# Second attention: the scores of a batch's first half, issued on TensorE directly behind the outputs of the preceding round

## The chip, the cores and the metric

The kernel runs on one core of one Trainium2 chip. The metric is the device time of one execution in microseconds (us), lower is better. The profile names the engines PE (TensorE matmuls), PEld (TensorE weight loads), DVE (VectorE), ACT (ScalarE), POOL (GpSimd) and SP (SyncE, which issues DMAs here).

## What is computed

Sixteen batches of 128 tokens with 128 features go through two layers, all in fp32. Each layer is a cross-attention over a context of 128 tokens and an expert layer, each behind a layer norm and a residual:

```python
x = x + xattn0(layernorm(x), ctx)      # 16 heads of 8
x = x + ffn0(layernorm(x))             # top 2 of 8 experts
x = x + xattn1(layernorm(x), ctx)      # 16 heads of 64, the "second attention"
x = x + ffn1(layernorm(x))             # 16 experts, each takes 32 tokens of a batch

def xattn1(x, context):                # low-rank terms are folded into the weights
    q_in = x @ Wq                      # 16 heads x 64
    org, ipa = context[:124], context[124:]
    out = attention(q_in, org @ Wk, org @ Wv) + attention(q_in, ipa @ Wk_ipa, ipa @ Wv_ipa)
    return out @ Wo + bo
```

The two attentions of the third line have softmaxes of their own, one over 124 context tokens and one over the last 4.

## The kernel before

Every engine has a program written out by hand, and waits on semaphores for the others; no scheduler reorders anything. The first attention runs from the start to about 139 us of the span, the second attention, together with the first expert layer and the router of the second, to about 393 us, and the second expert layer to the end.

The second attention is a loop of rounds, `round1(b)` for b = -1 to 16, on each engine in its own order. In round b TensorE works on three batches at once: the scores of batch b, the inputs of batch f = b+1 (queries, keys, values) and the end of batch t = b-1 (turning its probabilities, outputs, projection); beside these, one batch g = b+4 of the first expert layer. TensorE's order in round b before the change is: scores of the first half (L1510, heads 0 to 7, banks 0 and 1), turn 0 (L1521), queries 0 (L1530), turn 1, queries 1, expert block (L1463), scores of the second half (L1510, banks 2 and 3), turn 2, keys 0 (L1538), turn 3, expert block, outputs of both halves (L1551), keys 1, values 0 (L1558), inputs (L1564, a transpose), values 1, projection (L1721, bank 7). In rounds 1 and 5 a router of the first expert layer adds a turn (L1451) and logits (L1458) to the first part; in rounds 12 and 13 the second router adds blocks (L1570, L1576, L1583), and in rounds 15 and 16 the gathering of tokens does.

A `scores(b, half)` call is eight matmuls that take 64 rows of the array each, two side by side. It waits for the queries and keys of its half, for the four extra context tokens (`Z.ki`), and for the exponentials of batch b-1 that still read its banks (`Z.exp`).

VectorE's order in a round is: reduce the first quarter of the scores (`shifted(b, 0)`, L772 to L775), copy the turned tile 0 of batch t out of bank 4 (`turned(t, 0)`, L783), the second quarter, turned tile 1, small work on sums and statistics, the third quarter, turned tile 2, the fourth quarter, keys 0 (L919), turned tile 3, expert outputs (L745), the reciprocals and the norm of the four tokens; then it waits for the projection of batch t and does the residual (L306), its statistics (L310), in some rounds further normalizing (L698, L621), and the normalized tile xn of batch b+3 (L301). ScalarE does the exponentials (L1150) and copies queries, keys, outputs and values out of the banks. GpSimd scales the probabilities (L498), adds up the expert outputs (L481, L483) and adds the bias (L492).

Two waits of TensorE matter below. Queries 1 writes bank 4, so it waits until VectorE has copied turned tile 0 out of it; the second half of the outputs waits for turned tile 3:

```python
queries(f, 1, *((Z.p_sb, CH * t + 1) if there(t) else (Z.q_sb, 2 * f)))
...
outputs(t, 1, *p_copied(t, 3))
```

Of the kernel before, what the change touches and what calls it, by code (L numbers as in the profile page):

```python
# [37 lines left out]
def after(eng, sem, value):  # L38

    if not isinstance(value, int) or value >= 1:  # L40
        eng.wait_ge(sem, value)


def there(b):
    return not isinstance(b, int) or 0 <= b < B
# [6 lines left out]
def build_program(nc, T, out):  # L52

    with ExitStack() as ctx:
# [15 lines left out]
        def blocks(b_, rows=128):  # L70
            return b_[0:rows, :].rearrange("p (g n) -> p g n", g=CH)
# [217 lines left out]
        def p_copied(t, n):  # L289

            done = CH * min(t, LAST_TURNS) + 2 * max(t - LAST_TURNS, 0) + n + 1
            if t < LAST_TURNS:
                return Z.p_sb, done
            return (Z.p_odd, 2 * (t - LAST_TURNS) + n // 2 + 1) if n % 2 else (Z.p_sb, done - n // 2)

        def head_of(b):

            return {-1: 1, 1: 2, 5: 3}.get(b)
# [1029 lines left out]
        def _(pe):  # L1328
# [172 lines left out]
            def scores(b, half):  # L1501

                pe.wait_ge(Z.q_sb, 2 * b + half + 1)
                pe.wait_ge((Z.k0_sb, Z.k1_sb)[half], b + 1)
                pe.wait_ge(Z.ki, b + 1)
                after(pe, Z.exp, CH * (b - 1) + 2 * half + 2)
                for c in range(CH):
                    for odd in range(2):
                        rows = slice(D1 * odd, D1 * odd + D1)
                        mm = pe.matmul(blocks(bank[2 * half + odd])[:, c, :], q1T[rows, b % 2, CH * half + c, :],  # L1510
                                       k1T[rows, b % 2, CH * half + c, :], start=True, stop=True)
                        if c == CH - 1:
                            mm.then_inc(Z.score, 1)
# [27 lines left out]
            def outputs(t, n, freed, count):  # L1541

                for k in (2 * n, 2 * n + 1):
                    pe.wait_ge(*p_copied(t, k))
                pe.wait_ge(Z.v_sb, 2 * t + n + 1)
                pe.wait_ge((Z.vi0, Z.vi1)[t % 2], 16 * (t // 2 + 1))
                after(pe, freed, count)
                for c in range(CH):
                    for odd in range(2):
                        h = 8 * n + 2 * c + odd  # L1550
                        mm = pe.matmul(blocks(bank[5 - n])[D1 * odd:D1 * odd + D1, c, :], v1[:, t % 2, D1 * h:D1 * h + D1],  # L1551
                                       p1T[:, CH * (2 * n + odd) + c, :], start=True, stop=True)
                mm.then_inc(Z.o, 1)
# [12 lines left out]
            def route_turn(g, to):  # L1566

                pe.wait_ge(R.xn, 4 * g + 4)
                for k in range(4):
                    mm = pe.transpose(blocks(to)[:, k, :], xn_half[g // 2][:, 4 * (g % 2) + k, :], ident[:, :])  # L1570
                mm.then_inc(R.tr, 1)
# [40 lines left out]
            def round1(b):  # L1612
                f, t, g, j = b + 1, b - 1, b + 4, head_of(b)
                if b == 0:
                    pe.wait_ge(W.taken, ALL_TAKEN)
                    pe.wait_ge(W.added, ALL_ADDED)
                if there(b):
                    scores(b, 0)
                if there(t):
                    turn(t, 0, Z.o_sb, 2 * t)  # L1620
                if b == B:
# [60 lines left out]
                    gather(6)  # L1682
                if there(t):
                    outputs(t, 1, *p_copied(t, 3))
                if b == 12:
                    pe.wait_ge(R.h, 1)
                    route_turn(1, bank[7])
# [94 lines left out]
            for b in range(-1, B + 1):  # L1782
                round1(b)
# [95 lines left out]
```

## Time and profile before

| | |
|---|---|
| time, median of 3 runs | 515.21 us (513.41 to 516.83) |
| span of the profiled execution | 513.1 us |
| PE busy | 487.3 us, 95% of the span |
| DVE busy | 354.2 us, 69% |
| ACT busy | 288.2 us, 56% |
| POOL busy | 234.4 us, 46% |
| chain that ended last, by engine | PE 79%, DVE 12%, ACT 3% |

The page gives the profiled execution by its span, from its first to its last instruction, and no other time of it; the median of the three timed runs is 2.1 us above that span. The page has parts for busy time, for the span in slices, for the chain of work that ended last and for groups of instructions by line. The views used below are the chain in order of time (start, length, what; a piece ends where the next link starts, so its length is what it adds to the chain) and the timeline of one engine (start, length, engine, line, operation, tiles; neighbours of one line are merged, and idle time before a row stands behind it in brackets with what ended it).

### The profile page before, as it was taken

How to read it: one execution, taken by the hardware profiler on the slowest of the kernel's cores; microseconds unless marked ns; L12 is line 12 of the kernel's file. 1: busy time of each engine (PE TensorE's matmuls, PEld its weight loads, DVE VectorE, ACT ScalarE, POOL GpSimd, SP SyncE). 2: the span in 40 equal slices, each digit the busy share in tenths (PEclk: the TensorE clock that was granted, in tenths of full speed). 3: DMA queues.
4: the chain of work that ended last, by engine and by line, in shares of the span. 5: the costliest groups of instructions: out<-in, count | busy, mean ns of one | idle time of the engine just before them, and what ended most of it. 6: DMA issues, size and time to landing. Idle time of an engine off the chain costs nothing.

```text
span 513.1 us, 13570 instructions
## 1 busy us (share of the span) xinstructions
PE 487.3 (95%) x5109; PEld 378.7 (74%) x5113; DVE 354.2 (69%) x1000; ACT 288.2 (56%) x984; POOL 234.4 (46%) x331
## 2 busy tenths in 40 slices
PE   4799999998999999999999999899999999999996
PEld 3466766656668778887787777788757897799995
DVE  5888989766786678566786665757866588535553
ACT  3366566463586776666867657665664444413332
POOL 4845545035365544575444755324231980090440
PEclk9699999999999999999999999999999999999999
DMA  8900000000001100111000000022202100000001
GB/s 229 234 3 4 3 3 3 3 1 8 4 1 32 34 20 16 34 33 34 3 2 2 4 3 3 1 66 64 64 0 71 56 0 1 1 22 24 1 2 42
DMA packets 21872, 14.48 MB, mean 28 GB/s; under 512 B 5928, under 2 KB 21136, under 8 KB 21808
## 3 DMA queue, kind: packets, MB, share of 16 engines
q1 hardware_dynamic: 20704, 13.31, 9.6%
q8 instruction: 42, 0.69, 0.6%
q10 hardware_dynamic: 1104, 0.30, 0.3%
q14 instruction: 22, 0.18, 0.1%
HBM read 12.30 MB, written 1.05 MB: 26 GB/s over the span
## 4 chain that ended last, share of the span: by engine, by line
PE 79%; DVE 12%; ACT 3%; issue 2%; DMA 1%; POOL 1%; ACTq 0%; DVEq 0%; POOLq 0%
PE bank L1792 9%; PE bank L1721 6%; PE bank L1551 5%; PE bank L1558 5%; PE bank L1801 5%; PE bank L1538 5%; PE bank L1510 5%; PE bank L1374 5%; PE bank L1463 5%; PE bank L1521 4%; PE bank L1530 4%; PE bank L1808 3%; PE bank L1609 3%; PE bank L1359 3%; ACT work L1150 2%
## 5 line engine op out<-in xcount | busy, mean ns | idle before, releaser
L1150 ACT ACTIVATE work<-bank,negmax 128x124 f32<-128x124 f32 x256 | 90.0, 387 | 52.2 <-DVE ipa_s L775 52.0
L498 POOL TENSOR_TENSOR work<-work,rsum 128x496 f32<-128x496 f32 x64 | 64.1, 1012 | 120.2 <-DVE rsum L789 120.2
L533 POOL TENSOR_SCALAR work<-work,slot 128x128 f32<-128x128 f32 x64 | 49.7, 792 | 48.3 <-DVE slot L864 29.4
L1150 ACT ACTIVATION_READ_ACCUMULATOR work<-bank,negmax 128x1 f32 x256 | 58.9, 230 | 0.0
L1792 PE MATMUL bank<-work 128*128 128x256 f32 x224 | 53.4, 381 | 0.0
L1014 DVE SCALAR_TENSOR_TENSOR work<-work,bank 128x256 f32<-128x256 f32 x64 | 26.9, 421 | 33.0 <-ACT work L1302 32.8
L1302 ACT ACTIVATE work<-bank 128x256 f32<-128x256 f32 x64 | 24.5, 383 | 40.6 <-PE bank L1792 29.1
L481 POOL TENSOR_TENSOR work<-work 128x512 f32<-128x512 f32 (+2 forms) x48 | 39.2, 817 | 12.1 <-DVE work L745 9.6
L306 DVE TENSOR_TENSOR x_all<-bank,x_all 128x128 f32<-128x128 f32 x16 | 4.7, 292 | 57.4 <-PE bank L1721 55.4
L1792 PEld LDWEIGHTS bank<-work 128*128 128x128 f32 x224 | 40.3, 190 | 4.7 <-DVE work L1017 0.2
L773 DVE TENSOR_REDUCE negmax<-bank 128x4 f32<-128x496 f32 x64 | 42.5, 664 | 0.0
L432 POOL TENSOR_TENSOR rstd<-veps,minus_half 128x1 f32<-128x1 f32 (+3 forms) x28 | 21.2, 755 | 46.1 <-DVE veps L575 45.8
L783 DVE COPY work<-bank 128x512 f32<-128x512 f32 x60 | 40.9, 681 | 0.8 <-PE bank L1521 0.8
L1510 PEld LDWEIGHTS bank<-work 64*128 64x128 f32 x512 | 31.1, 187 | 13.9 <-ACT work L1157 7.6
L629 DVE TENSOR_REDUCE negmax<-bank 128x8 bf16<-128x1024 f32 x32 | 39.1, 1221 | 2.2 <-PE bank L1344 1.7
L1521 PE MATMUL bank<-ident,work 128*128 128x128 f32 x256 | 40.1, 279 | 0.1
L1510 PE MATMUL bank<-work 64*128 64x128 f32 x512 | 37.2, 285 | 1.1 <-issue 1.1
L1090 ACT ACTIVATE work<-bank 128x1024 f32<-128x1024 f32 x32 | 31.0, 1021 | 11.8 <-PE bank L1359 11.8
L1551 PEld LDWEIGHTS bank<-work 128*64 128x64 f32 x512 | 27.7, 136 | 13.5 <-issue 8.7
L1721 PEld LDWEIGHTS bank<-work 128*128 128x128 f32 x256 | 31.1, 192 | 7.4 <-ACT work L1163 5.4
L1530 PE MATMUL bank<-xT,work 128*128 128x128 f32 x256 | 34.3, 278 | 1.6 <-DVE work L783 1.4
L1538 PE MATMUL bank<-cT_all,work 96*128 96x124 f32 x256 | 35.1, 280 | 0.0
(197 smaller groups left out, 1101.1 us busy)
## 6 DMA issues: line engine op xcount, KB each, us to landing
work<-in_L_ffn_w_dram SPq DMA_DIRECT2D x42, 128.0 KB, 2.3
x_all<-in_x_dram SPq DMA_DIRECT2D x4, 256.0 KB, 5.8
out_dram<-x_all SPq DMA_DIRECT2D x4, 256.0 KB, 2.6
ctx_all<-in_ctx_dram SPq DMA_DIRECT2D x4, 192.0 KB, 6.0
ctx_all<-in_L_ffn_w_dram SPq DMA_DIRECT2D x6, 128.0 KB, 2.3
work<-in_L_xattn_Wq_dram SPq DMA_DIRECT2D x1, 512.0 KB, 6.5
work<-in_L_xattn_Wo_dram SPq DMA_DIRECT2D x1, 512.0 KB, 8.2
work<-in_L_ffn_We_dram SPq DMA_DIRECT2D x1, 512.0 KB, 5.7
```

Source lines behind the costliest of these rows:

```text
L498: pool.tensor_tensor(part, part, rsum1[:, b % 2, CH * n:CH * n + CH].unsqueeze(2).broadcast_to((128, CH, ORG)), ALU.mult).then_inc(Z.norm, 1)
L533: ins = pool.tensor_scalar(ohw_of(e)[:, k, :], count[:, :], slot[:, h, 0, k, e % E1:e % E1 + 1], slot[:, h, 1, k, e % E1:e % E1 + 1], ALU. ...
L773: dve.tensor_reduce(negmax1[:, b % 2, part], got_s[:, :, 0:ORG], X, ALU.max, negate=True)
L783: dve.tensor_copy(p1T[:, CH * n:CH * n + CH, :], blocks(bank[(4, 6, 5, 4)[n]])).then_inc(Z.p_sb, 1)
L1150: ins = act.activation(p1[:, b % 2, n, c, 0:ORG], blocks(bank[n])[:, c, 0:ORG], ACT.Exp, bias=negmax1[:, b % 2, h:h + 1], accum_out=sums1[ ...
L1510: mm = pe.matmul(blocks(bank[2 * half + odd])[:, c, :], q1T[rows, b % 2, CH * half + c, :], k1T[rows, b % 2, CH * half + c, :], start=True ...
L1521: mm = pe.transpose(blocks(bank[(4, 6, 5, 4)[n]])[:, c, :], p1[:, t % 2, n, c, :], ident[:, :])
L1530: mm = pe.matmul(blocks(bank[5 - n])[:, c, :], wq1[:, part], xT[:, f % 2, :], start=True, stop=True)
L1538: mm = pe.matmul(bank[6][:, ORG * c:ORG * c + ORG], wk1[0:C, part], cT_all[:, f, 0:ORG], start=True, stop=True)
L1551: mm = pe.matmul(blocks(bank[5 - n])[D1 * odd:D1 * odd + D1, c, :], v1[:, t % 2, D1 * h:D1 * h + D1], p1T[:, CH * (2 * n + odd) + c, :], s ...
L1721: mm = pe.matmul(bank[7][:, 0:D], o1T[:, c, :], wo1[:, c, :], start=(c == 0), stop=(c == 7))
L1792: mm = pe.matmul(halves(bank[4 + c])[:, n, :], up_weights(e, n, c), xgT[e // E1][:, :, e % E1, :], start=True, stop=True)
```

## The change

In rounds 1 to 15 the call `scores(b, 0)` no longer opens round b. It is made one round earlier, in round b-1, behind the second half of the outputs and ahead of the second block of keys. The scores of batch 0 stay where they were. No other engine's program is touched.

```diff
@@ def round1(b), TensorE @@
                 if b == 0:
                     pe.wait_ge(W.taken, ALL_TAKEN)
                     pe.wait_ge(W.added, ALL_ADDED)
-                if there(b):
-                    scores(b, 0)
+                    scores(0, 0)
                 if there(t):
                     turn(t, 0, Z.o_sb, 2 * t)
@@
                 if there(t):
                     outputs(t, 1, *p_copied(t, 3))
+                if f > 0 and there(f):
+                    scores(f, 0)
                 if b == 12:
                     pe.wait_ge(R.h, 1)
                     route_turn(1, bank[7])
```

TensorE's order from the outputs of one ordinary round (L1551) to the second queries block of the next (the second L1530), before the change; each row is a line, its operation and tiles, and how many matmuls:

```order
L1551 MATMUL bank<-work 64x128 x16
L1538 MATMUL bank<-cT_all,work 128x124 x4
L1558 MATMUL bank<-work,cT_all 124x512
L1564 MATMUL bank<-ident,xn 128x128
L1558 MATMUL bank<-work,cT_all 124x512
L1721 MATMUL bank<-work 128x128 x8
L1510 MATMUL bank<-work 128x128 x8
L1521 MATMUL bank<-ident,work 128x128 x4
L1530 MATMUL bank<-xT,work 128x128 x4
L1521 MATMUL bank<-ident,work 128x128 x4
L1530 MATMUL bank<-xT,work 128x128 x4
```

The same stretch after the change (the projection's line is L1722 there):

```order
L1551 MATMUL bank<-work 64x128 x16
L1510 MATMUL bank<-work 128x128 x8
L1538 MATMUL bank<-cT_all,work 128x124 x4
L1558 MATMUL bank<-work,cT_all 124x512
L1564 MATMUL bank<-ident,xn 128x128
L1558 MATMUL bank<-work,cT_all 124x512
L1722 MATMUL bank<-work 128x128 x8
L1521 MATMUL bank<-ident,work 128x128 x4
L1530 MATMUL bank<-xT,work 128x128 x4
L1521 MATMUL bank<-ident,work 128x128 x4
L1530 MATMUL bank<-xT,work 128x128 x4
```

The scores (L1510) moved up over keys, values, inputs and projection; all else keeps its order. VectorE's order around the same place, from the end of one round to the copy that the second queries block waits for, after the change (in brackets the semaphores that a row waits for):

```order
L798 TENSOR_TENSOR work<-ipa_s,ipa_sum 128x16x4 [waits z_ipa_step]
L306 TENSOR_TENSOR x_all<-bank,x_all 128x128 [waits z_xb,z_proj]
L310 BN_STATS stats<-x_all 128x6 [waits z_x_new]
L301 TENSOR_SCALAR xn<-x_all,mv,rstd 128x128 [waits z_tr,ln_rstd]
L772 TENSOR_REDUCE ipa_max<-bank 128x4 [waits z_score]
L773 TENSOR_REDUCE negmax<-bank 128x4
L775 TENSOR_TENSOR ipa_s<-bank,ipa_max 128x16 [waits z_ipa_max]
L783 COPY work<-bank 128x512 [waits z_turned]
```

Nothing moved here: all of VectorE's rows stand as before, the residual (L306) ahead of the scores' reduction (L772).

## Rows read from the trace of the kernel before

**Rows 1.** The page: the span, and busy time by engine.

```profile
span 513.1 us, 13570 instructions
PE 487.3 (95%) x5109; PEld 378.7 (74%) x5113; DVE 354.2 (69%) x1000; ACT 288.2 (56%) x984; POOL 234.4 (46%) x331
```

**Rows 2.** Chain of waits, round 8: start us, length us, what.

```profile
257.48 1.09 PE bank L1510 x16
258.57 0.59 PE bank L1521 x4
...
260.05 0.44 PE bank L1521 x4
260.49 0.89 PE bank L1530 x8
...
263.92 0.89 PE bank L1538 x8
...
266.11 1.90 PE bank L1551 x32
268.01 1.08 PE bank L1538 x8
...
270.93 1.79 PE bank L1721 x16
```

**Rows 3.** Timeline of VectorE, round 8: start us, length us, line, operation.

```profile
257.52 0.29 DVE L306 TENSOR_TENSOR x_all<-bank,x_all 128x128 f32<-128x128 f32 x1 [4.13 <-PE bank L1721]
...
258.06 0.37 DVE L301 TENSOR_SCALAR xn<-x_all,mv,rstd 128x128 f32<-128x128 f32 x1
258.61 0.18 DVE L772 TENSOR_REDUCE ipa_max<-bank 128x4 f32<-128x16 f32 x1 [0.18 <-PE bank L1510]
...
259.36 0.68 DVE L783 COPY work<-bank 128x512 f32<-128x512 f32 x1
...
266.04 0.68 DVE L783 COPY work<-bank 128x512 f32<-128x512 f32 x1
```

**Rows 4.** Chain of waits, the start of round 10.

```profile
287.96 0.02 issue
...
289.26 0.35 DVE xn L301
...
290.97 0.14 issue
291.10 1.13 PE bank L1530 x8
```

**Rows 5.** Chain of waits, round 7.

```profile
241.88 1.14 PE bank L1510 x16
243.02 0.16 DVE ipa_max L772
...
251.69 1.09 PE bank L1551 x16
```

**Rows 6.** Timeline of VectorE, ahead of round 1.

```profile
145.70 2.01 DVE L698 TENSOR_SCALAR work<-x_all,mv,rstd 128x128 f32<-128x128 f32 x2
```

**Rows 7.** Chain of waits, round 1.

```profile
148.31 0.44 PE bank L1451 x4
...
150.87 0.99 PE bank L1530 x8
```

**Rows 8.** Chain of waits, round 13.

```profile
337.53 1.09 PE bank L1510 x16
...
341.40 0.89 PE bank L1530 x8
```

**Rows 9.** Timeline of VectorE, round 14.

```profile
358.78 0.18 DVE L772 TENSOR_REDUCE ipa_max<-bank 128x4 f32<-128x16 f32 x1
```

**Rows 10.** Chain of waits, round 15.

```profile
370.22 2.87 ACT work L1150 x16
```

**Rows 11.** Timeline of GpSimd, round 8.

```profile
258.98 0.45 POOL L492 TENSOR_TENSOR x_all<-x_all,bias 128x128 f32<-128x128 f32 x1
```

## Prediction

> **What bounds the kernel now.** The page comes first: TensorE is busy for 95% of a 513.1 us span [rows 1]. A busy TensorE can still be waiting in disguise, so the chain of waits comes next. I read it over the second attention, where the change lies, and speak of round b from P, the end of the projection that closes round b-1, to the next P. In round 8 (257.48 to the next P, 272.72 = 270.93 + 1.79) every link is a TensorE block that starts when the one before it ends [rows 2]: 15.24 us without a gap. Each block's length is the distance to the next start.
>
> The blocks show a second thing. The first half's scores (L1510) take 1.09 us and the turn behind them 0.59 us, while the same turn behind whole-array work takes 0.44 us. Keys take 1.08 us behind the outputs and 0.89 us elsewhere [rows 2]. Scores use half the array's rows, outputs half its columns; each change of mode costs 0.15 to 0.2 us (0.59 - 0.44, 1.08 - 0.89).
>
> Then the timeline of VectorE in the same round [rows 3]. After P it takes the projection (L306), the statistics, the normalized tile xn (L301, from P + 0.58), and only then reduces the scores (L772, from 258.61, after 0.18 us of waiting for them) and copies the first turned tile (L783). That copy frees bank 4 for the second queries block (L1530 at 260.49). VectorE's order is fixed, and the change leaves it as it is. So today the scores on TensorE (1.09 us) and VectorE's residual and xn (0.9 us) run side by side. VectorE has no long wait until the next P: its last copy for the outputs starts at 266.04, near the outputs themselves.
>
> **What the change costs.** Its instruction count is nil: in rounds 1 to 15 the eight scores matmuls leave the round's head and stand, with their four waits, behind the outputs of the round before. I take head and tail apart.
>
> *Head.* TensorE loses 1.09 us and the 0.15 us of the following turn, 1.24 us. From P it now does turn, queries, turn: 0.44 + 0.89 + 0.44 = 1.77 us, and stands before the second queries block. That block waits for VectorE's copy. How long VectorE needs is shown where it is already the bound: in round 10 xn starts at 289.26 and the block at 291.10, 1.84 us later, with 0.14 us from the copy's end to the matmul [rows 4]. With xn at P + 0.58 the block can start at P + 2.42, not P + 1.77: a stall of 0.65 us. Before, it started at P + 3.01 (260.49 - 257.48). So the head gives 0.59 us, not 1.24. The first block behind such a stall also takes 1.13 us instead of 0.89 [rows 2, 4], 0.24 us more. What was hidden behind the scores (residual, statistics, xn) becomes visible, because the scores no longer stand there.
>
> *Tail.* The block now stands between outputs and keys, where TensorE is the only bound and nothing waits for a scores block: 1.09 us more, less what keys save by following scores (1.08 against 0.89 + 0.15): +1.05 us. No row shows outputs followed by scores. Below, I bound it by a block with no change of mode at all: 16 matmul records of the projection take 1.79 us one by one, the 16 of the scores run in pairs, so 0.90, and keys back at 0.89: +0.71. Above: 1.09 and 0.19 us for one more change (1.08 - 0.89): +1.28. I take 1.05, since scores and keys both have their own rows. Their waits cost nothing: the exponentials, queries and keys they need are all made earlier in the round.
>
> The rounds then are:
> - 2, 6, 8, 9: -0.59 + 0.24 + 1.05 = +0.70 each, 2.80.
> - 3, 7: VectorE is the chain through the round. In round 7 it starts on the scores at P + 1.14 (243.02 - 241.88), and only its last copy lets the outputs go (251.69) [rows 5]. Without the scores ahead it starts at P + 0.58 + 0.35 = 0.93 (the length of xn [rows 4]): -0.21 + 1.05 = +0.84 each, 1.68.
> - 4, 10, 11, 12: VectorE's extra work behind P (more normalizing, more statistics) already sets the second queries block, or the exponentials do; round 10's starts at P + 3.14 [rows 4]. The head gives nothing: +1.05 each, 4.20.
> - 1, 5: a router turn (L1451) in the head waits for VectorE's normalized inputs (L698). In round 1 these end at 145.70 + 2.01 = 147.71 [rows 6]. The turn started at 148.31 and the second queries at 150.87 [rows 7], 2.56 us apart: after the change, with 0.05 us for the handover (257.48 to 257.52 is 0.04 [rows 2, 3]), 147.71 + 0.05 + 2.56 + 0.24 = 150.56, 0.31 earlier. -0.31 + 1.05 = +0.74; I give round 5 the same: 1.48. Round 0's own small delay, from scores that now stand ahead of its keys, disappears in that wait.
> - 13: the head has one block more, so its second queries block (P + 3.87 [rows 8], against 3.01 in round 8) moves to P + 2.63, still behind VectorE's 2.42: the full gain, -1.24 + 1.05 = -0.19.
> - 14: VectorE reaches the third quarter of the scores (358.78) without idling before it [rows 9], so little of the head counts: +1.05. Rounds 15 and 16 have no new tail, and round 15's head is on the chain of VectorE and then ScalarE's exponentials [rows 10]: 0.
>
> Sum: 2.80 + 1.68 + 4.20 + 1.48 - 0.19 + 1.05 = **+11.0 us**. The span of 513.1 becomes 524.1. The median of the runs, 515.21, is 2.1 us above that span, so 526.2. With the tail at its two ends (14 tails) the time is 526.2 - 14 x 0.34 = 521.4, or 526.2 + 14 x 0.23 = 529.4.
>
> A next bound is close: VectorE's last copy. It ends in round 8 at about 266.04 + 0.60 = P + 9.16, and starts 0.2 us earlier after the change; the second outputs block would be reached at 2.42 + 1.13 + 4.73 (261.38, where second queries end, to 266.11) + 0.95 = P + 9.23, some 0.1 us behind it. Anything else late on VectorE will appear there.
>
> **A rule that speaks for the change.** The rows say that entering and leaving half-array work costs 0.15 to 0.2 us [rows 2]. The Trainium skill (TensorEngine Tiling (Array Packing), Key Properties) says that changing the tiling mode drains TensorE. By that rule alone a round would have five changes instead of six and be some 0.2 us shorter; the trace agrees with the price of a change, but not that TensorE's order alone will decide.
>
> **Rivals.**
> - *TensorE alone decides* (the other side: not slower). If the copy of the turned tile is ready by P + 1.77, each of 13 rounds gains 1.24 - 1.05 = 0.19 us: 515.2 - 2.5 = 512.7; with the tail at 0.71 it is 0.53 us, 508.3, more than 1% faster. For it: chains like round 8's are all TensorE, and no wait of VectorE is longer than 0.2 us there. Against: VectorE's 2.42 us behind P would have to be 0.65 us shorter, and no instruction of it moves. It decides if those 2.42 us fall below 1.77. The drain rule named above, taken alone, ends in this rival. Chance 0.07 within 1%, and 0.02 more for its faster end.
> - *VectorE gets slower behind P.* GpSimd's add of the bias (L492, 0.45 us) starts at 258.98, 0.92 us behind xn's start [rows 3, 11]. GpSimd follows VectorE's sums in the round, and the next P comes about 0.7 to 1 us later against them, so the two fall together. That xn-like work can suffer is shown in round 1: two L698 take 2.01 us [rows 6], against 0.35 for one such operation [rows 4]. At most 0.45 us in each of six rounds (2, 3, 6 to 9): +2.7, 528.9. Against: xn in round 8 runs while GpSimd is busy and takes 0.37. Chance 0.15. The Trainium skill (SBUF — State Buffer, SBUF: two separate sides) calls the port pair that VectorE and GpSimd share an exclusive lock; by it xn would wait out the whole add, which is this rival.
> - *The move does nothing*, since the new place lies in a wait that exists anyway. Then 515.2. Against: keys, values and projection follow the outputs without a gap in every chain row of the tail [rows 2]. Chance 0.03.
>
> **From these to numbers.** My forecast, 526, has 0.73. One per cent of 515.21, about what a measurement here can tell from no change, is 510.1 to 520.4. Faster by more holds only the far end of the first rival, 0.02; the rest of it and the third rival make 0.07 + 0.03 = 0.10 within 1%; the forecast and the second rival make 0.73 + 0.15 = 0.88 slower. For the range I leave out the first and third rival (0.12) and take the bounds of the tail, 521.4 and 529.4, widened by 1 us at each end for the rounds that I gave by analogy and for part of the second rival: 520.5 to 530.5.
>
> **What would show it.** In the changed profile, rounds 8 and 9 should be 15.9 us long, with TensorE idle 0.5 to 0.7 us before the second queries block, released by VectorE's L783; scores should start where the outputs end and take about 1.1 us. VectorE should no longer wait for the first half's scores at all. Rounds 4, 10 and 11 should grow by 1 us, round 13 not at all. I am wrong if no such stall stands there, if the scores block behind the outputs takes 0.9 us or less with keys at 0.9, or if the outputs wait for L783 in ordinary rounds too.

## The result and the profile after

The changed kernel takes 527.39 us (median of 4 runs, 526.59 to 527.71) against 515.57 us before (4 runs); the ratio is 1.0217, with a 95% interval of 1.0183 to 1.0251 (the quotient of the two medians, 1.0229, lies inside it). The forecast was 526.0 with a range of 520.5 to 530.5. The profiled execution has a span of 525.4 us and a time of 527.24 us, so 1.8 us lie around the span.

The page of the changed kernel, span and busy time by engine:

```profile
span 525.4 us, 13570 instructions
PE 491.2 (93%) x5109; PEld 380.7 (72%) x5113; DVE 352.0 (67%) x1000; ACT 288.3 (55%) x984; POOL 234.0 (45%) x331
```

The instructions are as many as before. TensorE is busy 3.9 us longer and the span grew by 12.3 us, so its share fell from 95% [rows 1] to 93%: most of the new time is time in which it waits. The chain of waits in round 8 (start us, length us, what), which stands against [rows 2] and [rows 3]:

```profile
262.98 1.80 PE bank L1722 x16
...
264.81 0.30 DVE x_all L306
...
265.34 0.36 DVE xn L301
...
265.79 0.58 DVE negmax L773
...
266.45 0.61 DVE work L783
267.06 0.14 issue
267.19 1.13 PE bank L1530 x8
...
273.06 1.90 PE bank L1551 x32
274.95 1.09 PE bank L1510 x16
276.04 1.08 PE bank L1538 x8
...
278.96 1.80 PE bank L1722 x16
```

Before, all of this was TensorE. Now the projection ends at P = 264.78, and the chain goes over to VectorE: residual (L306), xn (L301), reduction (L773), copy of the turned tile (L783). The second queries block starts 0.14 us behind that copy, at P + 2.41, and its length is 1.13 instead of 0.89 us. In the tail, the scores stand between outputs and keys with 1.09 us, and the keys behind them still take 1.08. The round is 15.98 us long (280.76 - 264.78), before 15.24. VectorE no longer idles before the first quarter's reduction: its first row (L772) starts at 265.63 while xn still ends, before it stood behind 0.18 us of waiting [rows 3].

TensorE's timeline shows the stall itself, and the list of waits its sum over rounds 2 to 14 (engine, line, what it waited for: us in total, times, longest):

```profile
267.19 1.13 PE L1530 MATMUL bank<-xT,work 128*128 128x128 f32 x8 [0.45 <-DVE work L783]
```

```profile
PE bank L1530 <- DVE work L783: 8.1, 11, 1.4
```

The idle time shown, 0.45 us, is shorter than the 0.64 us by which the block is late (2.41 against 0.44 + 0.89 + 0.44 = 1.77): the block in front is drawn to the end of its last matmul (0.60 us for a turn that takes 0.44 in the chain), 0.16 us or more beyond the point at which the next one could have started. The start times are the safer reading.

Lengths of the rounds, each from the end of a projection (start plus length of L1721 or L1722) to the next:

| round | before, us | after, us | longer by | forecast |
|---|---|---|---|---|
| 2, 6, 8, 9 | 15.25, 15.26, 15.24, 15.24 | 15.97, 16.15, 15.98, 15.95 | 0.72, 0.89, 0.74, 0.71 | 0.70 |
| 3, 7 | 15.62, 15.60 | 16.42, 16.43 | 0.80, 0.83 | 0.84 |
| 4, 10, 11, 12 | 15.67, 15.61, 16.29, 17.68 | 16.49, 16.70, 16.96, 18.36 | 0.82, 1.09, 0.67, 0.68 | 1.05 |
| 5 | 16.64 | 17.47 | 0.83 | 0.74 |
| 13 | 16.15 | 16.34 | 0.19 | -0.19 |
| 14 | 14.37 | 15.29 | 0.92 | 1.05 |
| 15 | 14.91 | 14.95 | 0.04 | 0 |
| sum of 2 to 15 | | | 9.93 | 10.28 |
| 0 and 1, to the end of round 1 | 163.44 | 165.85 | 2.41 | 0.74 |

9.93 + 2.41 = 12.34 us is the whole difference of the two spans (525.4 - 513.1 = 12.3).

### The profile page after: what moved, and what is told of

It is laid out like the page before. It is cut to its first block, busy times and chain, and to the rows that moved or that the text cites. A ratio compares the mean times of both kernels' runs of the same rounds, so it can differ in the third digit from the quotient of the medians.

```text
span 525.4 us, 13570 instructions
## 1 busy us (share of the span) xinstructions
PE 491.2 (93%) x5109; PEld 380.7 (72%) x5113; DVE 352.0 (67%) x1000; ACT 288.3 (55%) x984; POOL 234.0 (45%) x331
## 3 DMA queue, kind: packets, MB, share of 16 engines
HBM read 12.30 MB, written 1.05 MB: 25 GB/s over the span
## 4 chain that ended last, share of the span: by engine, by line
PE 79%; DVE 14%; issue 3%; ACT 2%; DMA 1%; SPq 0%; DVEq 0%
PE bank L1793 9%; PE bank L1510 6%; PE bank L1551 5%; PE bank L1722 5%; PE bank L1802 5%; PE bank L1538 5%; PE bank L1558 5%; PE bank L1374 5%; PE bank L1463 5%; PE bank L1530 4%; PE bank L1809 3%; PE bank L1359 3%; PE bank L1609 3%; PE bank L1521 3%; DVE work L783 2%
## 5 line engine op out<-in xcount | busy, mean ns | idle before, releaser
L498 POOL TENSOR_TENSOR work<-work,rsum 128x496 f32<-128x496 f32 x64 | 64.1, 1013 | 130.8 <-DVE rsum L789 130.8
L1150 ACT ACTIVATE work<-bank,negmax 128x124 f32<-128x124 f32 x256 | 90.2, 391 | 49.1 <-DVE ipa_s L775 49.1
L1150 ACT ACTIVATION_READ_ACCUMULATOR work<-bank,negmax 128x1 f32 x256 | 59.9, 234 | 0.0
L306 DVE TENSOR_TENSOR x_all<-bank,x_all 128x128 f32<-128x128 f32 x16 | 4.7, 291 | 72.7 <-PE bank L1722 69.6
L481 POOL TENSOR_TENSOR work<-work 128x512 f32<-128x512 f32 (+2 forms) x48 | 39.2, 817 | 12.1 <-DVE work L745 9.6
L1530 PE MATMUL bank<-xT,work 128*128 128x128 f32 x256 | 36.7, 288 | 8.1 <-DVE work L783 8.1
L1510 PEld LDWEIGHTS bank<-work 64*128 64x128 f32 x512 | 31.7, 190 | 14.9 <-ACT work L1157 7.6
L773 DVE TENSOR_REDUCE negmax<-bank 128x4 f32<-128x496 f32 x64 | 42.4, 662 | 0.0
L1530 PEld LDWEIGHTS bank<-xT,work 128*128 128x128 f32 x256 | 31.9, 196 | 13.0 <-issue 11.0
L783 DVE COPY work<-bank 128x512 f32<-128x512 f32 x60 | 40.7, 678 | 0.2 <-PE bank L1521 0.2
L1510 PE MATMUL bank<-work 64*128 64x128 f32 x512 | 37.8, 288 | 1.3 <-issue 1.3
L1551 PEld LDWEIGHTS bank<-work 128*64 128x64 f32 x512 | 27.7, 136 | 13.7 <-issue 8.7
L1722 PEld LDWEIGHTS bank<-work 128*128 128x128 f32 x256 | 31.1, 191 | 7.4 <-ACT work L1163 5.4
```

The source lines that it names most:

```text
L481: pool.tensor_tensor(y[:, 0:half, :], y[:, 0:half, :], y[:, half:2 * half, :], ALU.add).then_inc(F.sum, 1)
L498: pool.tensor_tensor(part, part, rsum1[:, b % 2, CH * n:CH * n + CH].unsqueeze(2).broadcast_to((128, CH, ORG)), ALU.mult).then_inc(Z.norm, 1)
L773: dve.tensor_reduce(negmax1[:, b % 2, part], got_s[:, :, 0:ORG], X, ALU.max, negate=True)
L783: dve.tensor_copy(p1T[:, CH * n:CH * n + CH, :], blocks(bank[(4, 6, 5, 4)[n]])).then_inc(Z.p_sb, 1)
L1150: ins = act.activation(p1[:, b % 2, n, c, 0:ORG], blocks(bank[n])[:, c, 0:ORG], ACT.Exp, bias=negmax1[:, b % 2, h:h + 1], accum_out=sums1[ ...
L1530: mm = pe.matmul(blocks(bank[5 - n])[:, c, :], wq1[:, part], xT[:, f % 2, :], start=True, stop=True)
```

## Experiments

All ratios are to runs of the kernel before that were taken along on the same chip. Lines of the experiments' kernels lie up to five further down than in the changed kernel, as their rows show. The rows are from the chain of waits (start us, length us, what) where nothing else is said.

**Only VectorE's reduction moved.** The changed kernel, in which VectorE reduces the next batch's first quarter of scores before it waits for the projection.

```diff
@@ round1(b), VectorE @@
-                if there(b):
+                if b == 0:
                     shifted(b, 0)
@@
+                if f > 0 and there(f):
+                    shifted(f, 0)
                 if there(t):
                     dve.wait_ge(Z.proj, t + 1)
```

> The changed kernel, with one thing moved on VectorE: it reduces the first quarter of the next batch's scores (L772 to L775) before it waits for the projection, no longer behind the residual and xn. Theory (VectorE's 2.4 us behind the projection hold the second queries block): the 0.83 us of that reduction leave the chain behind the projection, the copy of the turned tile is ready 1.7 us after it, before TensorE needs it at 1.77, and the stall is gone: ordinary rounds fall from 15.95 to about 15.1 us, rounds 3, 7, 10 to 12 and 14 by 0.8 us; some 10 us less, 516 to 519 us. Rival (the scores' new place itself costs, by the switch between half-array modes or by the banks): the stall before the second queries block goes but the time stays above 524 us. Rival (the lower clock around 135 us of the changed kernel's profile is what made it slower): no change, 527 us.

Measured: 517.67 us (10 runs), ratio 1.0034 (1.0009 to 1.0059), against 1.0217 for the changed kernel. An ordinary round's head, behind a projection that ends at 277.84:

```profile
277.84 0.44 PE bank L1523 x4
278.28 1.10 PE bank L1532 x8
279.38 0.44 PE bank L1523 x4
279.82 0.89 PE bank L1532 x8
```

The chain stays on TensorE, and the second queries block starts at P + 1.98 with its old length of 0.89. So the stall was VectorE's queue, and both rivals fall: nine of the eleven us come back without a change of the scores' place, and this profile too has a low granted clock (0.76) between 135 and 140 us. One thing was not in the forecast: the first queries take 1.10 instead of 0.89 us. With no scores ahead, TensorE reaches its wait for the residual (`Z.x_new`) before VectorE has done it.

**Only xn moved.** The changed kernel, with xn behind the copy of the turned tile.

```diff
@@ round1(b), VectorE @@
                 if there(t):
                     turned(t, 0)
+                if there(t) and there(t + 3):
+                    xn1_of(t + 3)
@@
-                if there(b + 3):
+                if there(b + 3) and b < 0:
                     xn1_of(b + 3)
```

> The changed kernel, with only VectorE's xn (L301, 0.33 us) moved from ahead of the first quarter's reduction to behind the copy of the turned tile. A part of the dose: by the theory the second queries block comes 0.33 us earlier in the rounds where it waits (2, 4, 6, 8 to 11), the stall in ordinary rounds falls from 0.65 to about 0.3 us and the time by 2.5 to 3 us, to 524.5 to 525. In rounds 3 and 7, where VectorE is the chain as a whole, nothing changes. If the stall is not VectorE's queue, the time stays at 527.4.

Measured: 525.15 us, ratio 1.0200 (1.0147 to 1.0252). The medians go the way expected, by 2.2 us where 2.5 to 3 were expected, but the intervals of this run and the changed kernel overlap, so the time alone settles nothing. The trace does, in a round whose P is 277.86:

```profile
277.88 0.30 DVE x_all L306
278.21 0.29 DVE stats L310
...
279.85 0.14 issue
279.98 1.13 PE bank L1532 x8
```

The block starts at P + 2.12 instead of 2.38 in the same round of the changed kernel (283.14 - 280.76 there): 0.26 us earlier for 0.33 us less in front. The rest is lost because the statistics (L310), whose end was overlapped by xn, now count whole. This is the best of the four ordinary rounds: rounds 2, 6 and 8 are 0.05, 0.21 and 0.14 us shorter than in the changed kernel.

**Only the tail.** The kernel before, with the scores done a second time behind the outputs, without telling anyone.

```diff
@@ the kernel before, TensorE @@
-            def scores(b, half):
+            def scores(b, half, told=True):
@@
-                        if c == CH - 1:
+                        if c == CH - 1 and told:
                             mm.then_inc(Z.score, 1)
@@ round1(b) @@
                     outputs(t, 1, *p_copied(t, 3))
+                if f > 0 and there(f):
+                    scores(f, 0, told=False)
```

> The kernel before, in which TensorE does the first half's scores twice: at the head of the round as before, and also behind the outputs of the preceding round, where nobody is told of them. It measures the tail alone, with the head as it was. Theory (a block there costs its full 1.05 to 1.09 us, no wait hides it): 14 tails, 515.6 + 15 = 530 to 531 us. Rival (between the outputs and the keys the change of mode is saved, 0.71 us a tail): 525.5. Rival (the place lies in a wait that exists anyway): 515.6.

Measured: 530.06 us, ratio 1.0301 (1.0246 to 1.0356): by the ratio 15.5 us on 515.1, 1.1 us for each of 14 tails; the two medians are 15.0 us apart and the two profiled spans 13.8. The tail in an ordinary round:

```profile
291.29 1.09 PE bank L1510 x16
292.38 1.08 PE bank L1538 x8
```

The block pays its full 1.09 us, no wait hides it, and the keys save nothing by standing behind scores: rounds 8 and 9 last 16.33 us, 1.09 more than before. Both rivals fall, and the forecast's tail of 1.05 was 0.04 too low. Rounds 4, 11 and 12 grow by clearly less here, by 0.83, 0.68 and 0.68 us, almost exactly as in the changed kernel, although the head is the old one; the section on the prediction comes back to them.

**The scores ahead of the projection.** The changed kernel, with the scores between the second values and the projection, so that whole-array work stands on both sides.

```diff
@@ round1(b), TensorE @@
-                if f > 0 and there(f):
-                    scores(f, 0)
@@
                     values(f, 1, Z.k1_sb, f + 1)
+                if f > 0 and there(f):
+                    scores(f, 0)
```

> The changed kernel, with the first half's scores put behind the second block of values, just ahead of the projection, and no longer behind the outputs. The stall of the second queries block is the same by the theory; the scores now have whole-array work on both sides, so that the number of changes of mode is as in the kernel before. If a change of mode costs 0.15 to 0.2 us, each of 14 rounds is that much longer than in the changed kernel: 529.5 to 530 us. If the direct neighbours (outputs, then scores) save nothing: 527.4.

Measured: 529.13 us, ratio 1.0282 (1.0227 to 1.0337), 0.65% or 3.3 us above the changed kernel's ratio, 0.24 us a round; the intervals of the two overlap a little. The rounds themselves say a little less: rounds 8 and 9 last 16.13 and 16.14 us against 15.98 and 15.95, 0.15 and 0.19 more. The rows name the place:

```profile
293.62 1.09 PE bank L1510 x16
294.71 2.00 PE bank L1722 x16
```

The projection takes 2.00 us behind scores, 1.80 elsewhere. So one more change between half-array and whole-array work costs 0.2 us, and outputs with scores directly behind them do save that much, as the forecast had it. The Trainium skill (TensorEngine Tiling (Array Packing), Key Properties) says that a change of tiling mode drains TensorE; these rows agree, and give 0.2 us for it here.

**Everything of VectorE that can go early.** The changed kernel, with the reduction, xn and the further normalizing and statistics ahead of the wait for the projection, and with TensorE's wait for the residual moved down to the expert block that needs it.

```diff
@@ round1(b), VectorE: ahead of the wait for the projection @@
+                if b in (-1, 3): head_input((b + 9) // 4, 0, 2)
+                if b in (0, 4): head_input((b + 8) // 4, 2, 4)
+                if f > 0 and there(f): shifted(f, 0)
+                ...      # variances of b = 9 and 13, normalize, slot_weights
+                if there(b + 3): xn1_of(b + 3)
                 if there(t):
                     dve.wait_ge(Z.proj, t + 1)
@@ round1(b), TensorE @@
-                after(pe, Z.x_new, t)
+                if j or b >= 12:
+                    after(pe, Z.x_new, t)
@@
+                if b < 12:
+                    after(pe, Z.x_new, t)
                 if there(g):
                     ...
                     ffn(g, 0, bank[7])
```

> The changed kernel, with VectorE's work that does not need the projection put ahead of its wait for it: the first quarter's reduction of the next batch, xn, and the further normalizing and statistics of rounds 0, 3, 4, 9 to 11, 13 and 14. Behind the projection only the residual, its statistics and the copy of the turned tile are left. TensorE's wait for the residual moves from ahead of the first queries to ahead of the expert block that needs it (rounds 0 to 11 without a router). Theory: the copy is ready 1.3 us behind the projection, TensorE decides alone, ordinary rounds take 15.24 - 0.19 = 15.05 us, rounds 3 and 7 about 15.3 instead of 15.6 before, 4, 10 and 11 about 15.1 instead of 15.7, 15.6 and 16.3: some 5 us less than the kernel before, 509 to 511 us. Rival (the scores' place behind the outputs is itself a loss): 515 or more.

Measured: 510.46 us (6 runs), ratio 0.9896 (0.9866 to 0.9925). It beats both kernels. Its round 9, with the head all on TensorE:

```profile
270.85 1.79 PE bank L1727 x16
272.63 0.44 PE bank L1523 x4
273.07 0.89 PE bank L1532 x8
273.96 0.44 PE bank L1523 x4
274.40 0.89 PE bank L1532 x8
...
285.93 1.78 PE bank L1727 x16
```

The round is 15.08 us (285.93 - 270.85), 0.16 less than before: what the move was worth once nothing waits, forecast as 0.19 and paid down by the tail's 0.04. (Rounds 4 and 10 to 12 gain more, from VectorE's new order, as the next run shows.) VectorE's timeline there:

```profile
268.71 1.16 DVE L301 TENSOR_SCALAR xn<-x_all,mv,rstd 128x128 f32<-128x128 f32 x1
272.67 0.29 DVE L306 TENSOR_TENSOR x_all<-bank,x_all 128x128 f32<-128x128 f32 x1 [2.80 <-PE bank L1727]
...
273.21 0.67 DVE L783 COPY work<-bank 128x512 f32<-128x512 f32 x1
```

The copy ends 1.2 us behind P (272.63), and VectorE still waits 2.80 us for the projection, so there was room for all of it.

**The same order of VectorE in the kernel before.** The diff is the VectorE part of the last one, without the reduction; TensorE is as in the kernel before.

> The kernel before, with the same work of VectorE put ahead of its wait for the projection, except the reduction of the scores, which in this order are not there yet. It tells how much of the version with everything early comes from VectorE's order alone. Theory: ordinary rounds stay at 15.24 us, since TensorE is their bound; rounds 4, 10 and 11, whose second queries wait for VectorE today, fall to 15.24: some 2 to 3 us less than the kernel before, 512 to 513 us. If VectorE's order is the whole gain, it equals the version with the moved scores.

Measured: 512.74 us (9 runs), ratio 0.9946 (0.9926 to 0.9965). Its round 9:

```profile
270.44 1.78 PE bank L1721 x16
272.23 1.09 PE bank L1510 x16
...
285.67 1.79 PE bank L1721 x16
```

15.23 us, as before. So VectorE's order alone is worth half a per cent, out of the rounds that waited for it. The intervals of this run and the one above just touch (0.9925 and 0.9926): the scores' new place, with its two companions (the early reduction on VectorE and the later wait of TensorE), gives about another 0.5%. In the two profiles rounds 2 to 15 last 216.30 us here and 213.94 us there, 2.36 apart, and 1.39 of that stand in round 15 alone (14.74 against 13.35). Round 15's chain runs over VectorE's reduction and ScalarE's exponentials; with the reduction done early, eight of these (1.49 us) stand in the chain instead of sixteen (2.88). So less than half of that gain is the 0.16 us an ordinary round. (The two spans differ by 1.0 us only, since round 1 ends 1.4 us later in the other profile, 164.86 against 163.49.)

**TensorE's wait for the residual left early.** As the version with everything early, with the changed kernel's `after(pe, Z.x_new, t)` ahead of the first queries.

> The version with VectorE's free work ahead of the projection wait, but with TensorE's wait for the residual left where the changed kernel has it, ahead of the first queries. It splits that version's gain. In the run with only the reduction moved, the first queries took 1.11 instead of 0.89 us, since with no scores ahead TensorE reaches that wait before the residual is done. Theory: the same 0.2 us stand in rounds 2 to 4 and 6 to 11, which take 15.3 instead of 15.1 us: about 2 us more than the version with the late wait, 512 to 513 us. If the wait costs nothing, 510.5.

Measured: 513.97 us (12 runs), ratio 0.9956 (0.9934 to 0.9979). An ordinary round's start and end:

```profile
273.99 1.79 PE bank L1724 x16
...
276.21 1.11 PE bank L1532 x8
...
289.29 1.78 PE bank L1724 x16
```

15.30 us, 0.22 more than with the late wait, and the 0.22 stand in the first queries (1.11 instead of 0.89). With that wait kept, the move of the scores gains nothing over VectorE's order alone (0.9956 against 0.9946). The median is 3.5 us above that of the late wait, where about 2 were expected, and outside the 512 to 513 us forecast. In the two profiles rounds 2 to 15 differ by 1.8 us (215.74 against 213.94), as expected; the rest is not explained by the wait: in this profile round 1 already ends 2.1 us later (166.96 against 164.86), and its clock is low from an earlier point on (0.94 between 100 and 130 us).

**The changed kernel once more**, for a second profile, since rounds 0 and 1 were 1.7 us longer than forecast.

> The changed kernel once more, for a second profile. In its first profile TensorE's granted clock was 0.59 to 0.71 between 135 and 140 us, and rounds 0 and 1 were 2.5 us longer than before where 0.7 was forecast; the kernel before had its low stretch in the first 60 us. If the low stretch there is a matter of the single execution, it is gone or elsewhere here, and rounds 0 and 1 are 0.7 to 1 us longer than before. If the change brings it, it is there again.

Measured: one run, 526.61 us, span 524.8. The low stretch is there again, and round 1 ends at 165.12 us, 1.68 later than before. Busy time and granted clock of 135 to 140 us (stretch, PE, PEld, DVE, ACT and POOL busy, then the clock as a share of 2.4 GHz, DMA): first in the kernel before, then in the changed kernel's first profile, then in this second one, then in the version with only xn moved, then in the kernel before with VectorE early:

```profile
135.00:140.00 5.00, 4.84 (x50) 3.99 (x50) 2.34 (x11) 2.80 (x15) 2.14 (x5) 1.00 0.01 3
```

```profile
135.00:140.00 5.00, 4.97 (x33) 4.57 (x34) 2.27 (x10) 2.31 (x12) 1.54 (x4) 0.66 0.01 3
```

```profile
135.00:140.00 5.00, 5.00 (x34) 4.48 (x34) 2.28 (x10) 2.30 (x12) 1.51 (x4) 0.66 0.01 3
```

```profile
135.00:140.00 5.00, 5.00 (x51) 4.00 (x48) 2.56 (x12) 3.38 (x18) 1.66 (x4) 1.00 0.01 3
```

```profile
135.00:140.00 5.00, 5.00 (x35) 4.02 (x34) 2.27 (x10) 3.71 (x19) 1.01 (x1) 0.73 0.01 3
```

The low stretch stands in both profiles of the changed kernel, but also in a kernel with TensorE's old order (0.73), and not in the version with only xn moved, which has the changed kernel's order on TensorE (1.00). So the moved scores do not bring it. It comes behind a wait of 1 us that every one of these programs has at about 134 us, in some of the profiles and not in others. What decides that is open.

## Why the prediction was right

**The head** was right in mechanism and size. It said P + 2.42 for the second queries block; rounds 8 and 9 show 2.41 and 2.38. The restart at 1.13 instead of 0.89 us came as read from [rows 4]. Moving VectorE's reduction away removed the stall, and moving xn away shortened it, which shows the cause.

**The tail** was sized at 1.05 us, between 0.71 and 1.28. It measured 1.09, with 1.08 for the keys behind it: keys save nothing there. That is 0.04 us a round, 0.6 in all.

**Rounds 3 and 7** came within 0.04 us of the forecast, and the list of rounds was right in kind: nothing in round 15, the least in round 13.

**Rounds 4, 11 and 12** were forecast 0.2 to 0.4 us too long. The step that failed is that VectorE's extra work behind P keeps its length. It did not. These rounds grow by as little in the run with only the tail, whose head is the old one, so it is the later projection and not the head that shortens them. In round 11 the four normalizing operations, before and after the change, on VectorE's timeline before and in the chain after:

```profile
304.14 1.51 DVE L621 TENSOR_SCALAR work<-x_all,mv,rstd 128x128 f32<-128x128 f32 x4
```

```profile
313.97 1.10 DVE work L621 x4
```

Their length follows GpSimd, as the rival said, but with the other sign. P comes later against GpSimd's work, so that GpSimd's additions (L481, L483) are over when the normalizing starts. GpSimd's timeline before (round 11's P being 303.57) and in the changed kernel (P being 313.41):

```profile
301.76 2.61 POOL L481 TENSOR_TENSOR work<-work 128x512 f32<-128x512 f32 x3
```

```profile
310.50 2.62 POOL L481 TENSOR_TENSOR work<-work 128x512 f32<-128x512 f32 x3
313.19 0.46 POOL L483 TENSOR_TENSOR x_all<-x_all,work 128x128 f32<-128x128 f32 x1
```

The long ones (L481) end at 313.12; before they ended at 304.37, 0.8 us behind P and 0.23 us behind the start of the normalizing. In every run with scores behind the outputs or ahead of the projection in which the normalizing still follows P, the four operations take 1.09 or 1.10 us. That GpSimd is the cause is read from these times; no run moved GpSimd's work alone. The rival's own case appeared once in rounds 2 to 13, in round 6, where VectorE's xn met a memset of GpSimd's second router (timelines of VectorE and of GpSimd):

```profile
232.76 1.02 DVE L301 TENSOR_SCALAR xn<-x_all,mv,rstd 128x128 f32<-128x128 f32 x1
```

```profile
232.65 1.06 POOL L519 MEMSET work<- 128x1152 f32 x1
```

That is 1.02 us instead of 0.36, and part of round 6's 0.89. The bias addition (L492), which the rival had named, cost next to nothing. It did meet xn in round 8 (265.17 to 265.63, xn from 265.34), but only 0.29 us of it were left by then, and xn takes 0.36 us there, where it was 0.37 before.

**Round 13** was forecast at -0.19 and came at +0.19. The step that failed is the pure TensorE sum of its head: the router's block ran into the wait for the residual, 1.07 instead of 0.86 us, which is 0.21 of the 0.38 us:

```profile
349.16 1.07 PE bank L1576 x2
```

It is the wait that later held the first queries of the experiments.

**Rounds 0 and 1** were forecast at 0.74 and came at 2.41. The step that failed is the head of round 1, put at -0.31: the low clock and a collision on VectorE stand there, and neither was reckoned with. The low clock is a smaller part of it than it looks: the scores of batch 0's second half start 1.5 us later (140.56 instead of 139.10), but ScalarE's exponentials behind them (L1150) only 0.54 later (142.62 instead of 142.08), since the chain of the kernel before ran over ScalarE there, and not over TensorE. Another 0.74 come up to the router's turn (L1451, 149.59 instead of 148.31), and 1.13 in the rest of round 1, where 1.05 was forecast for the tail. The 0.74 go back to a race between VectorE and GpSimd. The two engines' timelines in the first profile of the changed kernel, then in the second:

```profile
146.21 1.04 DVE L798 TENSOR_TENSOR work<-ipa_s,ipa_sum 128x64 f32<-128x64 f32 x1
146.16 1.99 POOL L498 TENSOR_TENSOR work<-work,rsum 128x496 f32<-128x496 f32 x2
```

```profile
146.13 0.23 DVE L798 TENSOR_TENSOR work<-ipa_s,ipa_sum 128x64 f32<-128x64 f32 x1
146.15 2.05 POOL L498 TENSOR_TENSOR work<-work,rsum 128x496 f32<-128x496 f32 x2
```

The program is the same. Where VectorE's L798 (the norm of the four extra tokens) starts 0.05 us behind GpSimd's L498 (the scaling of the probabilities) it takes 1.04 us; where it starts 0.02 ahead it takes 0.23, and round 1 ends 0.73 us earlier. All ten profiles fall into these two cases. How long these rounds are in the changed kernel at full clock was not seen. The nearest run is the one with only xn moved, at full clock and with L798 at 0.23 us: from the first scores to the end of round 1 it takes 28.89 us, 0.61 more than before (28.28), near the 0.74 forecast.

The errors partly cancelled: 9.93 instead of 10.28 us in rounds 2 to 15, and 1.7 us too little ahead of them. The first rival, TensorE alone, is what the ordinary rounds of the version with everything early became: 0.16 us a round, once VectorE's 2.4 us behind the projection were cut to 1.2. The rule on tiling modes was right on its price, and would have given the wrong sign for this change by itself.

## What to carry to other kernels

Before moving a block on the engine that is the bound, look at what the other engines do while it runs: a block can be the cover for a chain on another engine, and taking it away uncovers that chain while its own cost is paid in full at the new place. Measure that chain from a round in which it is already the bound, and move it as well; here the same move lost 2.2% alone and gained about half a per cent on top of VectorE's reordering, more than half of it in one round whose chain runs over VectorE and ScalarE. A wait that stood behind the moved block counts too: left in place, it took the gain back.

## What the runs showed of the hardware

A change between half-array and whole-array work on TensorE cost about 0.2 us here (a projection of 2.00 instead of 1.80 us), and the first block behind a stall 0.24 us beyond it (second queries of 1.13 instead of 0.89 us).

VectorE's normalizing operation (SBUF to SBUF, fp32, 128x128) takes 0.33 us, and up to 1.02 or 1.16 us beside GpSimd's work, here beside a memset too, which reads nothing. The Trainium skill (SBUF — State Buffer, SBUF: two separate sides) calls the port pair of the two an exclusive lock, and the memset case agrees with it: xn starts 0.11 us behind the memset and ends at 233.78, the memset at 233.71. Which of the two starts first can decide 0.8 us: VectorE's L798 took 0.22 or 0.23 us in the six profiles in which it started 0.02 to 0.07 us ahead of GpSimd's L498, and 1.04 us in the four in which it started 0.04 to 0.05 behind.

The place of TensorE's low clock differs between the profiles: behind the same wait of 1 us the granted clock between 135 and 140 us was 0.66 to 0.76 of 2.4 GHz in six of them and 1.00 in four; in the first 60 us it was 0.91 in the kernel before and 1.00 in the changed kernel.
